# The gates' last product in three fp32r passes, with its weights split by GpSimd

## The reference, cut to what matters

```python
def _gate(h, q, Wg, bg, Wq, bq):          # B = 8 batches, L = 64 queries, N = 32 nodes a batch, F = 768
    hg = jnp.einsum('bnf,gf->bng', h3, Wg[:, :F])
    qg = jnp.einsum('blf,gf->blg', q, Wg[:, F:]) + bg
    attn = jax.nn.sigmoid(hg[:, :, None, :] + qg[:, None, :, :])
    qi = jnp.einsum('bnlf,blf->bnf', attn, q)
    alpha = jax.nn.sigmoid(jnp.einsum('bnf,gf->bng', h3, Wq[:, :F]) + jnp.einsum('bnf,gf->bng', qi, Wq[:, F:]) + bq)
    hn = alpha * jnp.tanh(qi) + (1.0 - alpha) * h3
```

## Time and profile before

| | us |
|---|---|
| median of 3 runs | 1113.02 (1111.66 to 1113.74) |
| the profiled execution | 1112.59 |
| its span | 1110.8 |
| PE busy | 1062.8 (96%) |
| DVE busy | 765.7 (69%) |
| ACT busy | 569.6 (51%) |
| GpSimd busy | 182.4 (16%) |

### The profile page before, as it was taken

The page is one execution under the profiler, slowest core; times in us unless marked ns, Lnnn a source line. Parts: engine busy times, 40 slices in busy tenths (PEclk is TensorE's granted clock), DMA queues, the critical chain, the costliest instruction groups (busy, mean ns, idle before and its releaser), DMA issues.

```text
span 1110.8 us, 17503 instructions
## 1 busy us (share of the span) xinstructions
PE 1062.8 (96%) x7372; PEld 882.2 (79%) x7372; DVE 765.7 (69%) x1089; ACT 569.6 (51%) x600; POOL 182.4 (16%) x100
## 2 busy tenths in 40 slices
PE   6999999999999999999999989899999999999987
PEld 5889986454799974456689689758999999999984
DVE  8894755888643158886454665656888888888852
ACT  0433226888433268884233544325666666666630
POOL 3525602555100015552000000000000000000000
PEclk9999999999999999999999999999999999999999
DMA  8142286122044372220244004408877777777720
GB/s 290 13 165 92 86 273 169 58 58 58 1 171 171 123 231 70 61 58 1 86 171 171 29 1 171 167 1 297 256 245 254 243 254 245 256 253 255 256 87 29
DMA packets 82290, 163.18 MB, mean 147 GB/s; under 512 B 4044, under 2 KB 60136, under 8 KB 81918
## 3 DMA queue, kind: packets, MB, share of 16 engines
q1 hardware_dynamic: 80736, 151.86, 40.9%
q0 software_dynamic: 1472, 10.15, 3.4%
HBM read 158.35 MB, written 0.80 MB: 143 GB/s over the span
## 4 chain that ended last, share of the span: by engine, by line
PE 79%; DVE 13%; issue 4%; ACT 2%; DMA 1%; POOL 1%; SPq 0%; DVEq 0%; POOLq 0%; ACTq 0%
PE PS L1059 19%; PE PS L743 8%; PE PS L911 7%; PE PS L759 5%; PE PS L665 4%; PE PS L1042 4%; PE PS L1073 4%; PE PS L484 4%; PE PS L641 3%; PE PS L554 3%; PE PS L497 3%; PE PS L566 3%; PE PS L799 2%; PE PS L976 2%; DVE PRD L1627 1%
## 5 line engine op out<-in xcount | busy, mean ns | idle before, releaser
L1873 DVE TENSOR_TENSOR Wlo<-W,Whi 128x2304 fp32r<-128x2304 f32 x68 | 173.7, 2556 | 43.4 <-ACT Whi L1383 43.4
L1383 ACT CAST Whi<-W 128x2304 fp32r<-128x2304 f32 x68 | 144.4, 2126 | 0.0
L1059 PE MATMUL PS<-Whi,Mhi 128*128 128x384 f32 x408 | 137.9, 338 | 0.0
L1059 PE MATMUL PS<-Wlo,Mhi 128*128 128x384 f32 x408 | 136.5, 334 | 0.0
L1059 PE MATMUL PS<-Whi,Mlo 128*128 128x384 f32 x408 | 136.4, 334 | 0.0
L456 POOL TENSOR_TENSOR PRDP<-arena 128x1024 f32<-128x1024 f32 x48 | 114.7, 2389 | 112.9 <-PE PS L759 84.1
L743 PE MATMUL PS<-QH,SEL 128*128 128x512 f32 x384 | 115.7, 422 | 5.2 <-ACT xT L1230 1.4
L1251 ACT ACTIVATE arena<-PS 128x1024 f32<-128x1024 f32 x96 | 98.4, 1025 | 23.5 <-PE PS L743 23.5
L743 PEld LDWEIGHTS PS<-QH,SEL 128*128 128x128 f32 x384 | 64.8, 188 | 55.0 <-DVE PRD L1627 21.2
L1251 ACT ACTIVATE PS<-PS 128x1024 f32<-128x1024 f32 x96 | 98.0, 1021 | 2.6 <-PE PS L743 2.6
L1059 PEld LDWEIGHTS PS<-Whi,Mlo 128*128 128x128 f32 x408 | 76.8, 188 | 0.0
(11 more groups left out here) (288 smaller groups left out, 2367.2 us busy)
## 6 DMA issues: line engine op xcount, KB each, us to landing
W<-in_L_rel SPq DMA_DIRECT2D x68, 1152.0 KB, 5.6
W<-in_W_rel SPq DMA_DIRECT2D x6, 2304.0 KB, 8.5
W<-in_W SPq DMA_DIRECT2D x6, 2304.0 KB, 8.4
arena<-in_qU SPq DMA_DIRECT2D x96, 128.0 KB, 2.6
W<-in_WqT SPq DMA_DIRECT2D x4, 2304.0 KB, 9.2
W<-in_W_root SPq DMA_DIRECT2D x2, 2304.0 KB, 13.5
W<-in_WgT SPq DMA_DIRECT2D x2, 2304.0 KB, 9.0
QH<-QH POOLq DMA_DIRECT2D x2, 1536.0 KB, 9.8
```

The costliest lines, as they stand in the source:

```text
L1059: mm = pe.matmul(PS[:, 4 + s % 2, 0:HALF], MS[a][mb][:, k, j * P:(j + 1) * P], WS[b][w % 3][:, k, :], start=n == 0, stop=n == 17)
L1383: nc.scalar.copy(WS[0][w % 3][:], W[(FIRST34 + r) % 2][:, :, q * HALF:(q + 1) * HALF]).then_inc(w_hi, 1)
L1873: V.tensor_tensor(WS[1][w % 3][:], W[(FIRST34 + r) % 2][:, :, q * HALF:(q + 1) * HALF], WS[0][w % 3][:].bitcast(F32), ALU.subtract).then_i ...
```

## The change

- PE: `alpha_part` makes three fp32r passes for each block, with the weights' rounded part in WH and the residue in WR (in W's own place), and qi's rounded part and residue in QIS[0] and QIS[1]. It first waits for all 30 pieces (wq_split).
- qi: ACT copies each turned bank to the rounded part (`sums_high`), DVE subtracts it from the bank and writes the residue, in the place of the copy to qiT.
- GpSimd: `split_piece(g, n)`, n = 0 to 29, by turns a rounded copy and a residue. Pieces 0 to 5 are 512 columns (two k of the first third), all others 256. Eight are made ahead of a gate's loop, the others one by one behind the products k = 1 to 22.
- GpSimd: the five bias loads come after both gates (w_used 15); DVE's wait for them moves from before the layer norm into `gcn_out(1)`.
- Gate 1: the split of W_root2's second third moves behind the three gate parts, on ACT and on DVE; QIS lies in part in its buffer.

```diff
-        qiT, tanhT = put("qiT", [P, KC, NODES], F32, 100)[:], MT[0][:]
+        tanhT = MT[0][:]
+        QIS = [[put(f"QI{x}{j}", [P, 2, NODES], F32R, at + 2 * j) for j in range(3)] for x, at in (("hi", 100), ("lo", 84))]
@@ gpsimd
-            pool.wait_ge(wr_used, 3 * (R3 + 1))
-            for i, n in enumerate(("b_gcn", "L1_b", "L2_b1", "L2_b2", "b_rgcn")):
-                pool.dma_start(biasN[:, i, :], A[n].partition_broadcast(P)).then_inc(small_in, 16)
+            def split_piece(g, n):
+                m = 7 * g + 7
+                if n == 0:
+                    pool.wait_ge(w_in[m % 2], 16 * (m // 2 + 1))
+                if n < 6:
+                    q, ks = 0, slice(n // 2 * 2, n // 2 * 2 + 2)
+                else:
+                    i = (n - 6) // 2
+                    q, ks = 1 + i // 6, slice(i % 6, i % 6 + 1)
+                whole, high = third_turned(W[m % 2], q)[:, ks], WH[q][:, ks]
+                if n % 2 == 0:
+                    nc.gpsimd.tensor_copy(high, whole).then_inc(wq_split, 1)
+                else:
+                    pool.wait_ge(wq_split, 30 * g + n)
+                    nc.gpsimd.tensor_tensor(third_turned(WR[m % 2], q)[:, ks], whole, high.bitcast(F32), ALU.subtract
+                                            ).then_inc(wq_split, 1)
                 pool.dma_start(QH[1][64:P], QH[0][64:P]).then_inc(hg_copied, 16)
+                for n in range(8):
+                    split_piece(g, n)
...
                     nc.gpsimd.tensor_tensor(PRDP[k % 2], SIGP, QD[h], ALU.mult).then_inc(pool_prod, 1)
+                    if 1 <= k < 23:
+                        split_piece(g, k + 7)
+
+            pool.wait_ge(w_used, 15)
+            for i, n in enumerate(("b_gcn", "L1_b", "L2_b1", "L2_b2", "b_rgcn")):
+                pool.dma_start(biasN[:, i, :], A[n].partition_broadcast(P)).then_inc(small_in, 16)
@@ tensor
-                Wq2 = W[(m0 + 6) % 2]
+                pe.wait_ge(wq_split, 30 * (g + 1))
...
+                    Wq2 = (WH[m // 2], third_turned(WR[(m0 + 6) % 2], m // 2))
                     for k in ks:
-                        mm = pe.matmul(PS[:, m // 2, (m % 2) * NODES:(m % 2 + 1) * NODES], Wq2[:, k, m * P:(m + 1) * P], qiT[:, k, :],
-                                       start=k == 0 and m % 2 == 0, stop=k == KC - 1 and m % 2 == 1, skip_group_check=True)
+                        for a, b in ((0, 0), (1, 0), (0, 1)):
+                            mm = pe.matmul(PS[:, m // 2, (m % 2) * NODES:(m % 2 + 1) * NODES], Wq2[b][:, k, m % 2, :],
+                                           QIS[a][k // 2][:, k % 2, :], start=k == 0 and a == b == 0 and m % 2 == 0,
+                                           stop=k == KC - 1 and b == 1 and m % 2 == 1, skip_group_check=True)
@@ scalar
+                def sums_high(j):
+
+                    act.wait_ge(qi_turned, 3 * g + j + 1)
+                    nc.scalar.copy(QIS[0][j][:], PS[:, 4 + j, :].rearrange("p (k n) -> p k n", k=2)).then_inc(qi_hi, 1)
+
+                sums_high(0)
+                sums_high(1)
                 for j in range(3):
+                    if j == 2:
+                        sums_high(2)
                     act.wait_ge(qiT_copied, 3 * g + j + 1)
...
                 if g == 0:
                     third_hi_turned(0)
-                    third_hi_turned(1)
                 for j in range(3):
...
+                if g == 0:
+                    third_hi_turned(1)
@@ vector
-                    dve.wait_ge(qi_turned, 3 * g + j + 1)
-                    V.tensor_copy(qiT[:, 2 * j:2 * j + 2, :], PS[:, 4 + j, :].rearrange("p (k n) -> p k n", k=2)).then_inc(qiT_copied, 1)
+                    dve.wait_ge(qi_hi, 3 * g + j + 1)
+                    V.tensor_tensor(QIS[1][j][:], PS[:, 4 + j, :].rearrange("p (k n) -> p k n", k=2), QIS[0][j][:].bitcast(F32),
+                                    ALU.subtract).then_inc(qiT_copied, 1)
...
                 if g == 0:
                     third_lo_turned(0)
-                    third_lo_turned(1)
...
+                if g == 0:
+                    third_lo_turned(1)
                 rest = PS[:, 5, :].rearrange("p (t f) -> p t f", t=NT)
...
             def gcn_out(n, bias):
 
+                if n == 1:
+                    dve.wait_ge(small_in, SMALL)
...
-            dve.wait_ge(small_in, SMALL)
             normalise(1)
```

More of the change, by code:

```diff
@@ L268, in build @@
         pool_prod = sem("pool_prod")
+        wq_split, qi_hi = sem("wq_split"), sem("qi_hi")
         qi_copied, qi_turned, qiT_copied, tanh_done = sem("qi_copied"), sem("qi_turned"), sem("qiT_copied"), sem("tanh_done")
```

## The result

The changed kernel takes 1108.82 us, the median of 5 runs (1106.78 to 1109.07), against 1112.83 for the kernel before (5 runs, 1111.66 to 1113.74). The ratio is 0.9965, 95% interval 0.9955 to 0.9976: faster by 0.35%, more than the 0.2% from which a change of this kernel counts. Run again beside the experiments, the ratio was 0.9975 (0.9965 to 0.9985). Over all runs the kernel before has a mean of 1112.4 us (98 runs) and the changed kernel of 1109.1 (16 runs), 3.3 us less. Three executions of all these took 1179 us or more, far off all others, and stand in no median or mean of this text.

What follows compares the result with a forecast made beforehand. PE carries 79% of the chain, but a ring of PE, ACT and DVE paces the loop. Terms -1.7 - 0.97 - 1.2 + 0.4 = -3.5 us from 1112.59, plus 0.43 to the median, gave 1109.5 us, own range 1108.3 to 1110.7 (60%).

Steps and rivals of the forecast that it cites:

- Gate 2's tail: Behind gate 2's loop, limited by PE: cheaper fp32r passes, less the added ACT copy of qi, give -1.7 us.
- Bias loads: Moved behind both gates, they stop delaying the W load that PE awaits ahead of gate 1: -1.2 us, bounds 0 and -1.2.
- Gate 1's tail: Behind gate 1's loop, limited by DVE: one weight split fewer before the first sum, -0.97 us, bounds 0 and -1.7.
- The moved split's wait: Gate 1's tail: PE waits 0.7 us for W_root2's later-split second third, in place of part of the gain.
- The loop: GpSimd's pieces behind 22 products a gate leave the ring standing with small delays: +0.4 us for both gates.
- Rival 1: In the loops, a piece takes the port before DVE's product: 0.45 us per eight steps, +9.9 us, so 1119; chance 12%.
- Rival 2: GpSimd overfull in the loops (copy 0.6, residue 1.0 us), its products slip and delay DVE: +2.2 us, 1111.7; chance 15%.
- Rival 3: W load stays late or DVE bounds gate 1's tail: one gain missing, 1110.5 to 1110.9, both 1111.7; chance 13%.

Runs made afterwards that it cites:

- The fp32 run: Changed kernel with the gate product as one fp32 pass over the residues, all splits and waits left in: 1111.14 us.
- the filler's run: Changed kernel with eight bf16 matmuls into a free PSUM bank ahead of TensorE's wait for Tlo's last third in gate 1's tail: 1109.05 us.
- both splits early: Changed kernel with residues of the sums placed elsewhere, so both halves of W_root2's second third are split ahead of gate 1's sums: 1109.26 us.

## Why the prediction was right, point by point

- **1109.5 us forecast, 1108.8 measured**, 1109.1 over all runs; -3.5 against -3.3 to -4.0.
- **Gate 2's tail, -1.7: right in kind, -1.99 measured.** The mis-sized term is the old product's record. I took 0.212 us from a row of weight loads; the chain gives 16.02 / 72 = 0.2225, 0.76 us more for the product. The new passes were sized too small as well, 12.96 against 13.42 in the chain, 0.46 more. The three groups lose 2.60 instead of 2.32, so the two errors hid each other in part. The fp32 run shows the same 2.60. The added ScalarE copy cost 0.61, forecast 0.63.
- **Bias loads, -1.2: the wait is gone, -1.27 to -1.37 in the stretch**, in every kernel that moves them. What they bring alone in the total the runs don't resolve. In the new place there is less room than I reckoned with: the last load took 12.5 us and landed at 542.36, the bias sum started at 542.39, and its releaser in the trace is this load (in the second profile it came 0.4 us after DVE was free). It costs nothing, since after the bias sum DVE still idles for 6.02 us:

```profile
542.39 1.76 DVE L1756 TENSOR_TENSOR xN<-xN,biasN 128x1536 f32<-128x1536 f32 x1
550.17 1.02 DVE L1763 SCALAR_TENSOR_TENSOR xN<-PS,dinv,xN 128x768 f32<-128x768 f32 x1 [6.02 <-PE PS L507]
```

- **Gate 1's tail, -0.97: -1.31 without the fall (the filler's run), -0.37 with it.** The chain of DVE went as worked out: its last sum started at 302.05, 20.86 us behind the last GpSimd product, where the forecast has 302.9 - 281.81 = 21.1. The moved split's wait was sized 0.7 and measures 0.3. What the forecast had no term for is the clock: 0.94 us, or 0.97 by the run with the piece ahead of the product. So gate 1's term holds only as the sum of a gain that was larger and a loss that was not foreseen.
- **The loop, +0.4: nothing.** The order of GpSimd and DVE at the port was right, but I let part of the wait fall on DVE. It fell on GpSimd alone, whose pieces read 1.73 and 1.44 us, inside its idle time. In work a residue took 0.73 (0.83 taken) and a copy 0.40.
- **Rival 1** priced a round at 0.45 us. The run with the piece ahead of the product, another way to bring the piece in first, shows 0.6 to 0.7. **Rival 2** was far: some 1.0 us more in eight steps cost only 0.05 to 0.08 us a round. **Rival 3** would have been right for gate 1 with both splits early (37.65 against 37.88).
- So the small error of the sum is partly luck: at a full clock the three stretches give -1.37 - 1.31 - 1.99 = -4.7, 1.2 us more than the -3.5 that I worked out, and the clock took 0.9 of it back in both profiles of the changed kernel. The loop's +0.4, which wasn't needed, stood on the other side.

## What to carry to other kernels

Cut both traces at the same instructions and subtract before you explain anything; unchanged stretches then show how much chance there is, here up to 1.5 us, nearly half of the gain. Price an operation from rows of the chain, not from the weight loads beside it. Work for an idle engine that shares a port can be free when it is queued behind that engine's own urgent work and fits into its idle time; here the same pieces ahead of it cost 14 us, and some 1.0 us more of them in eight steps lengthened each loop by 0.6 to 0.8.

## What the hardware showed that I had not expected

- **The granted clock falls for 3.4 or for 6.8 us**, and no other length stands in the fourteen profiles besides a fall at the very end, where TensorE has finished. It fell behind idle stretches of TensorE, but their length doesn't decide. In all fourteen it fell behind the 2.4 to 2.9 us at the last branch, and also ahead of the attention, where in thirteen the longest idle stretch of the nine microseconds before is 0.5 us (1.5 in the other). In gate 1's tail it fell behind 1.84 to 1.87 us in four profiles (the changed kernel twice, without the pieces, with the extra copies) and not behind 1.84 and 1.86 in two (both splits early, the piece ahead of the product). With 0.9 of the 1.84 us filled it stayed at 1.00 in three of three; with two unfilled ones that stayed up as well, this speaks for the filler and doesn't prove it.
- **Length and place of a fall are worth 1.0 to 1.8 us each time**: from the last sums to the last product 6.8 to 7.1 us with the long fall and 5.5 to 5.8 with the short one; from gate 2's rows to the last sums 529.3 to 529.5 instead of 527.7 to 528.3, where the fall ahead of the attention is long or late. Most of a single run's scatter can be this: the kernel before has a mean of 1111.7 us in the 50 runs whose granted clock over the whole run is 0.995, 1113.0 in the 34 with 0.994 and 1114.1 in the 9 with 0.993. That a kernel gets one or the other by its own timing is suggested by repeats (the kernel before twice long, the changed one twice short), but the kernel with the bias loads alone moved had one of each.
- **A port conflict makes the late one's record long, and leaves no idle time.** Copies of 0.40 us read 1.44, and GpSimd was busy 33 us longer in 100, of which only some 12 are work (an estimate: 11 residues of 0.73 and 11 copies of 0.40). The Trainium skill (SBUF — State Buffer, section SBUF: two separate sides) calls the lock exclusive for a whole instruction. The runs agree in both directions: DVE's product reads 1.23 us by itself and 2.10 when it comes late, GpSimd's residue 0.73 and 1.73.
